# Attention in a fused attention and expert kernel: the second key block's value products moved behind the second half's scores

## What is computed

```python
xn = layernorm(x)
# attention: 16 heads of 8 numbers, causal
q, k, v = split(xn @ in_proj.T)
a = einsum('bhtd,bhkd->bhtk', q / sqrt(8), k) + causal_mask
y = einsum('bhtk,bhkd->bhtd', softmax(a), v)
attention = y @ out_proj.T
# experts: one shared, seven routed, the two best of them for each token
ffn = shared(xn) + sum over the two chosen experts of weight * expert(xn)
out = x + attention + ffn
```

## Time and profile before

| what | value |
|---|---|
| median of 3 runs | 466.35 us (466.12 to 467.24) |
| profiled execution | 465.75 us, its span 464.0 us |
| PE busy | 431.9 us, 93% |
| PEld busy | 323.9 us, 70% |
| DVE busy | 360.9 us, 78% |
| ACT busy | 315.1 us, 68% |
| POOL busy | 295.4 us, 64% |
| granted TensorE clock | 0.998 of full speed |
| the two groups of value products (L976, L979), busy | 40.9 and 26.4 us |

### The profile page before, as it was taken

One profiled execution on the slowest core, in us unless ns is written; L12 is line 12 of the kernel. 1 busy time (PEld: TensorE's weight loads), 2 busy tenths in 40 slices (PEclk: granted clock), 3 DMA queues, 4 the chain that ended last, 5 costly groups with the idle time before them and its releaser, 6 DMA issues.

```text
span 464.0 us, 12501 instructions
## 1 busy us (share of the span) xinstructions
PE 431.9 (93%) x3983; PEld 323.9 (70%) x3987; DVE 360.9 (78%) x802; ACT 315.1 (68%) x709; POOL 295.4 (64%) x423
## 2 busy tenths in 40 slices
PE   8888898989899999999888999999999999999995
PEld 3766556656666666666666577888888888887783
DVE  5885999999878887877777077777777777776986
ACT  2756777767677777777676866666767776666552
POOL 1425888788888888888888900447457588775200
PEclk9999999999999999999999999999999999999999
DMA  8777799999875666655549226768868867822762
GB/s 232 225 226 256 199 378 292 296 325 353 283 247 159 172 188 173 184 161 153 154 114 335 69 59 181 255 195 279 288 210 279 282 209 258 270 92 68 254 182 70
DMA packets 60415, 99.84 MB, mean 215 GB/s; under 512 B 11045, under 2 KB 29226, under 8 KB 59328
## 3 DMA queue, kind: packets, MB, share of 16 engines
q1 hardware_dynamic: 55872, 90.57, 62.1%
q0 software_dynamic: 4480, 8.47, 5.5%
HBM read 60.85 MB, written 38.94 MB: 215 GB/s over the span
## 4 chain that ended last, share of the span: by engine, by line
PE 62%; DVE 13%; POOL 5%; ACT 4%; issue 3%; SPq 2%; DMA 1%; DVEq 0%; POOLq 0%; ACTq 0%
PE ps L846 12%; PE ps L847 12%; PE ps L848 12%; DVE sb_blockmax L1345 7%; PE ps L915 5%; PE ps L976 5%; PE ps L923 4%; ACT sb_work L702 3%; POOL xs L592 3%; PE ps L1145 3%; POOL sb_work L616 2%; PE ps L996 2%; PE ps L1134 2%; PE ps L979 2%; SPq L475 1%
## 5 line engine op out<-in xcount | busy, mean ns | idle before, releaser
L1345 DVE TENSOR_REDUCE sb_blockmax<-ps 128x6 f32<-128x768 f32 x128 | 121.5, 956 | 30.1 <-PE ps L923 24.4
L702 ACT ACTIVATE sb_work<-ps 128x768 f32<-128x768 f32 x128 | 104.4, 815 | 55.5 <-PE ps L911 54.2
L644 POOL DMA_INDIRECT ys<-sb_v_all,sb_xn_all x76 | 80.0, 1053 | 64.0 <-DVE sb_v_all L1466 46.4
L616 POOL TENSOR_SCALAR_AFFINE_SELECT sb_work<-sb_work 128x512 f32<-128x512 f32 x128 | 82.5, 646 | 24.9 <-ACT sb_work L702 23.2
L847 PE MATMUL ps<-sb_ring,sb_wb 128*128 128x512 f32 (+5 forms) x231 | 83.1, 360 | 0.0
L592 POOL DMA_INDIRECT xs<-sb_xn_all,sb_posu x64 | 62.8, 981 | 10.7 <-issue 10.7
L1444 DVE TENSOR_TENSOR sb_v_all<-ps,sb_v_all 128x512 f32<-128x512 f32 (+3 forms) x93 | 57.3, 616 | 14.1 <-ACT sb_v_all L793 9.9
L915 PE MATMUL ps<-sb_ring 32*128 32x256 f32 x256 | 49.2, 374 | 13.0 <-ACT sb_work L702 7.2
L793 ACT ACTIVATE sb_v_all<-ps 128x512 f32<-128x512 f32 (+3 forms) x93 | 49.8, 535 | 6.2 <-PE ps L848 5.4
L915 PEld LDWEIGHTS ps<-sb_ring 32*128 32x128 f32 x256 | 25.4, 181 | 36.6 <-issue 33.1
L846 PE MATMUL ps<-sb_ring,sb_wb 128*128 128x512 f32 (+1 forms) x138 | 50.8, 368 | 0.0
(11 more groups left out here) (165 smaller groups left out, 1071.3 us busy)
## 6 DMA issues: line engine op xcount, KB each, us to landing
sb_wb<-wd SPq DMA_DIRECT2D x50, 384.0 KB, 4.3
sb_ring<-qk SPq DMA_DIRECT2D x64, 256.0 KB, 3.4
wd<-sb_wb SPq DMA_DIRECT2D x8, 1088.0 KB, 6.0
sb_wb<-wd SPq DMA_DIRECT2D x25, 320.0 KB, 3.4
xs<-sb_o_all SPq DMA_DIRECT2D x19, 260.0 KB, 3.7
qk<-sb_ring SPq DMA_DIRECT2D x32, 128.0 KB
sb_work<-ys SPq DMA_DIRECT2D x16, 256.0 KB, 3.3
sb_xn_all<-xs SPq DMA_DIRECT2D x15, 260.0 KB, 3.6
```

The lines of the kernel that those rows point to most:

```text
L616: pool.affine_select(out=o, in_=o, compare_op=ALU.is_ge, fill=0.0, base=0, pattern=[[0, 4], [1, 128]], channel_multiplier=-1)\
L644: pool.indirect_dma_start(out=ys_d, out_offset=bass.IndirectOffsetOnAxis(ap=row, axis=0), in_=yst[i % NYS][:, EMB * j:EMB * j + EMB], in_o ...
L702: act.activation(part.rearrange("p (k h q) -> p h k q", h=2, q=128), ps[:, 4:6, 0:HEAD].rearrange("p h (k q) -> p h k q", q=128), ACT.Exp, ...
L1345: dve.tensor_reduce(blockmax[:, a:b + 1, 0:3], ps[:, a:b + 1, 0:HEAD].rearrange("p h (k c) -> p h k c", c=128), AX.X, ALU.max).then_inc(s[ ...
```

## The change

`sums(n)` becomes `value_sums(n, block)`. Block 0 keeps the waits and the four matmuls of the first key block and stays where `sums` stood, in front of the second half's scores. Block 1, the four matmuls of the second key block with the rise of `PV`, stands behind the second half's scores. No instruction is added, removed or altered.

```diff
-            def sums(n):
+            def value_sums(n, block):
                 b, j = quad(n)
-                if isq(n + 2):
-                    pe.wait_ge(s["q4b"], n + 3)
-                pe.wait_ge(s["sel"], 2 * n + 2)
-                pe.wait_ge(s["va"], b + 1)
                 p = P[n % 2].rearrange("p (a k h q) -> p a h k q", a=2, h=2, q=128)
-                for h in range(4):
-                    pe.matmul(J[32 * h:32 * h + 32, 256:512], v_sb[b % 2][:, 0, 4 * j + h, :],
-                              p[:, h // 2, h % 2, 1:3, :], start=True, stop=False, skip_group_check=True)
-                for h in range(4):
-                    last = pe.matmul(J[32 * h:32 * h + 32, 384:512], v_sb[b % 2][:, 1, 4 * j + h, :],
-                                     p[:, h // 2, h % 2, 0, :], start=False, stop=True,
-                                     skip_group_check=True)
-                last.then_inc(s["PV"], 1)
+                if block == 0:
+                    if isq(n + 2):
+                        pe.wait_ge(s["q4b"], n + 3)
+                    pe.wait_ge(s["sel"], 2 * n + 2)
+                    pe.wait_ge(s["va"], b + 1)
+                    for h in range(4):
+                        pe.matmul(J[32 * h:32 * h + 32, 256:512], v_sb[b % 2][:, 0, 4 * j + h, :],
+                                  p[:, h // 2, h % 2, 1:3, :], start=True, stop=False, skip_group_check=True)
+                else:
+                    for h in range(4):
+                        last = pe.matmul(J[32 * h:32 * h + 32, 384:512], v_sb[b % 2][:, 1, 4 * j + h, :],
+                                         p[:, h // 2, h % 2, 0, :], start=False, stop=True,
+                                         skip_group_check=True)
+                    last.then_inc(s["PV"], 1)
...
                 if isq(n - 1):
-                    sums(n - 1)
+                    value_sums(n - 1, 0)
                 if isq(n) or isq(n + 3):
                     scores(n, 1)
+                if isq(n - 1):
+                    value_sums(n - 1, 1)
                 if n > -4:
                     bank_read(n - 1)
```

## The result

The changed kernel takes **474.19 us** (median of 4 runs, 472.82 to 476.82) against 466.24 us (4 runs) before: ratio 1.0171, 95% interval 1.0137 to 1.0205, 7.9 us slower. The forecast was 471.6, its range 465.8 to 475.8. A second set of four runs of the changed kernel, on a chip with runs of before beside it, gave 473.13 against 465.99 (1.0150, 1.0100 to 1.0201). Medians leave out one execution that, at a lower clock, took over 1.5% more than the fastest of its kernel (474.11 us in run two).

What follows compares the result with a forecast made beforehand. The attention loop's step length on PE was taken as the bound, a ring through ACT deciding the plain step. Loop terms summed to 3.0 to 6.7 us; 5.3 on 466.35 gave 471.6, range 465.8 to 475.8.

Steps and rivals of the forecast that it cites:

- the late scores come sooner: Second half's scores on PE: start 0.22 us sooner behind L976, at 0.57 instead of 0.79.
- second ring: Late scores, L963, ACT's copies, exponential, next late scores: 2.69 us in the plain step, hidden before, lengthened by 0.51.
- PE's own queue: PE's instructions in order: grows 0.29 us a step, 0.21 at the lower price; 3.13 in the plain step.
- The price of a block: Four middle loop steps: 13.99 us at the upper price, 13.67 at the lower, against 13.50; +0.49 or +0.17.
- the upper price: Mask to L963 with both added changes of array form: 0.91 us at most, 0.51 later than before.
- The lower price: Mask to L963 only 0.43 us later, as 0.08 of L961's 0.25 to L963 may be gone.
- point 2: Four matmuls behind the mask add two changes of array form: mask to L963 0.51 us later at most, or 0.43.
- the DVE term: Five early blocks: DVE waits up to 0.45 us in the j = 0 step; 1.7 to 2.5 in all.
- the j = 3 step: Step with the turned sequence: 3.35 us after against 3.62, longer steps taking up the waits for POOL.
- The faster one: Rival: changing array form costs PE nothing behind the mask, at most 18 waits shrink: 463.5 us, chance 0.09.
- No change: Rival: form changes cost near 0.1 to 0.15 us in all, plain steps' gain pays: 466.3, chance 0.10.
- The much slower one: Rival: each drain lasts a matmul's full 0.27 us, 0.32 more a step: 479 us, chance 0.11.

Runs made afterwards that it cites:

- run two: Kernel before plus four one-column value products directly behind L979, beside others of their array form: 467.63 us, ratio 1.0017.
- runs three: Changed kernel with the second block's products between the late scores and their mask instead of behind the mask: 467.22 us, ratio 1.0024.
- ten: Kernel before with the second block's products between late scores and mask, and ACT's values' copy a step earlier: 464.68 us, ratio 0.9974.
- runs one: Kernel before plus four one-column value products behind the late scores' mask, adding two changes of array form: 471.32 us, ratio 1.0118.
- Run five: Changed kernel with the second block's products behind the side product, still in front of the maxima: 473.82 us, ratio 1.0159.
- run seven: Changed kernel with ACT's copy of a sequence's values made one step earlier: 469.65 us, ratio to before 1.0068.
- the fourth: Changed kernel with the first block's products moved behind the late scores' mask too: 501.23 us, ratio 1.0733.
- the ninth: Changed kernel with the second block's products behind the maxima (L963) at the step's end, output wrong: 465.19 us, ratio 0.9975.

## Why the forecast held, point by point

**The way it goes: right.** That the late scores come sooner was right (L976 to L915 falls from 0.79 to 0.57 where nothing is waited for, as in the plain steps of runs three and ten), and that it is worth little too: the wait for the exponentials fell from 6.1 to 0.3 us, and the kernel is slower. In the plain step the four products in their new place put L963 0.56 further behind the mask: 0.22 of work and 0.33 of changes of form, the second found with hardly any work in runs one and two. The Trainium skill says in "TensorEngine Tiling (Array Packing)", section Tiling Modes, that changing the mode drains TensorE. These runs agree in that each change costs time; the page has no number, and here it is 0.10 us up to L980's start and 0.13 behind it, with 0.1 more up to L963.

**The bound of the step: right.** The second ring sets the steps of the middle, as the table of its three distances shows. Two experiments separate it from PE's own queue: all products behind (35 us slower with a shorter queue) and the values' copy taken out (3.5 us faster with the same queue). Two more say which part counts: behind the maxima the kernel is as fast as before, behind the side product nothing is gained. In the plain step the two lie close: 3.26 by the ring, and PE's queue was put at 3.13.

**The price of a block: under-sized, and this is what the forecast lacks.** The prediction had 0.17 to 0.49 us a block of four middle steps and took a sum nearer the upper end; measured are 14.22 - 13.50 = 0.72. From late scores to late scores the four steps last 3.92, 3.61, 3.26 and 3.43, where the upper price gave 3.87, 3.57, 3.20 and 3.35. Mask to L963 is 0.96, not 0.91 at most: L980 to L961 takes 0.35 and not the 0.33 of the loop's end, L961 to L963 0.28 and not 0.25. The lower price, by which 0.08 of L961's distance to L963 would be gone behind L980, is not borne out: that distance grew. So the term that was mis-sized is the bound in point 2, 0.51 at most, with 0.56 measured; times four, 0.2 us a block. With it even the upper price was too low, 13.99 for 14.22, and the sum was taken below it. Seven blocks gave 5.0 us where 1.2 to 3.4 was written, and the middle stretch 99.5 us where 96 to 98 was to show it.

**The early blocks: right in size, wrong in cause.** 2.3 us against 1.7 to 2.5. From late scores to late scores it is the j = 0 steps that grew, by 0.36 each (3.55 to 3.92), and the j = 2 steps by 0.13; those of j = 1 and 3 did not. The j = 0 step was to grow because DVE waits up to 0.45 for the side product. But 3.92 is the length of the second ring, as in the middle (1.69 + 1.27 + 0.96). Run five, with the side product back in its early place, leaves it at 3.92, and run seven, which takes the values' copy out of that ring, brings it down to 3.61. So the DVE term is not borne out, the second ring sets these steps too, and it was chance that the sums agree. (From L976 to L976 the same growth shows in the j = 3 steps, 3.18 to 3.45, since the L976 that ends them comes later while the late scores behind it don't.)

**The rest.** Part ahead of the loop -0.6 (nothing written, no instruction is moved there), first three steps 0.33 (0.4 to 0.5 written), last twelve 0.62 (-0.3 to 0.3 written; the steps of j = 0 there are 3.56, with the values' copy in the ring, against 3.36 before), after the loop -0.4. The sum over the second profile is 7.3, above the 6.7 that the sum's upper end gave; the loop alone grew by 8.3, and the parts around it, in which nothing was moved, hide 1.0 of that. POOL's waits fell as foreseen (`PE L976 <- POOL` from 1.4 to 0.2 us). But the j = 3 step did not get shorter, as the prediction had it: its 3.62 is step 47 alone, the mean of the seven is 3.37, and it is 3.43 now.

**The rivals.** The faster one, a change of form for nothing, fell to runs one and two. No change (466.3) lies below both sets of runs. The much slower one (479) overstated the drain.

## What to carry to other kernels

Before moving work across a point where another engine is released, write down every ring that passes the two places, not only the one that is to be relieved: the work leaves one and enters another, and here the other ring was only 0.5 us below the bound in the plain step (2.69 against 3.20). In this kernel, matmuls that use the array in another form than their neighbours belong beside others of their form, or at a boundary where the form changes anyway: the same four matmuls cost 3.5 to 4.6 us in one place, 5 ahead of the mask and 11 to 12 behind it. A cheap relief is to look for what an engine could do in its regular idle time and does inside the ring instead, like the copy of the values.

## What the runs showed of the hardware

By the starts around L980, a change between the full array and the form of 128 rows by 32 columns costs 0.10 us of PE on the way in and 0.13 on the way out, about as much as the four products of 128 columns do in one pass (0.11). Up to L963 the two changes together cost 0.33 in the plain step, since L961 stands 0.15 behind the mask in one order and 0.35 behind L980 in the other, and L963 follows it after 0.25 and 0.28. Why L961 may start so soon behind the mask was not tested. Four one-column products placed between full-array matmuls cost 0.27 us up to the next start and 0.37 up to L963, beside others of their form 0.04.

The half clock was not expected in a kernel whose matrix engine is over 90% busy: it came in the changed kernel's first profile from the late scores of step 0 on, which follow a wait of 1.09 us, in the second run's behind a stretch in which PE stood 2.85 us for a transfer, and in those of the fourth and the ninth. The wait alone does not bring it: the profile of before has the same one (1.10 us at 45.27) and stays at full clock, and in the ninth run's the fall comes 1.8 us behind it. It cost about 3.8 us where it lasted some 10 us in the loop.
